# First adjacency blocks cast in halves by two engines, and engine programs outside a block, in a graph convolution with residual layer norm

## The reference

```
def reference(x, adj, t, weight):            # x 4096x256, adj 4096x4096, weight 256x256, all float32
    support = x @ weight
    y = (1 - t) * support + t * (adj @ support)
    return layernorm(x + y)                  # over the 256 features, eps 1e-5
```

## Time and profile before

| | |
|---|---|
| median of 3 runs | 384.52 us (384.37 to 384.85) |
| profiled execution, its own time | 384.54 us |
| its span, first to last instruction | 382.8 us |
| PE busy | 376.0 us (98%) |
| DVE busy | 238.5 us (62%) |
| ACT busy | 145.7 us (38%) |
| POOL busy | 22.4 us (6%) |
| moved by DMA | 84.42 MB, mean 221 GB/s |

### The profile page before, as it was taken

The page is one execution under the profiler, slowest core; times in us unless marked ns, Lnnn a source line. Parts: engine busy times, 40 slices in busy tenths (PEclk is TensorE's granted clock), DMA queues, the critical chain, the costliest instruction groups (busy, mean ns, idle before and its releaser), DMA issues.

```text
span 382.8 us, 4178 instructions
## 1 busy us (share of the span) xinstructions
PE 376.0 (98%) x1686; PEld 309.9 (81%) x1686; DVE 238.5 (62%) x335; ACT 145.7 (38%) x114; POOL 22.4 (6%) x19
## 2 busy tenths in 40 slices
PE   8999999999999999999999999999999999999994
PEld 5788888888888888888888888888888888888883
DVE  4958965446879467744577346873377643697315
ACT  4757544233352433323424324244332334523002
POOL 1201400003000010000100001000100001000000
PEclk9999999999999999999999999999999999999998
DMA  8999996556465756556655565756647567321001
GB/s 253 415 410 417 415 422 260 193 206 219 174 234 200 262 193 250 181 218 263 220 193 206 205 232 212 252 188 217 223 164 274 181 260 274 123 98 55 2 0 56
DMA packets 19107, 84.42 MB, mean 221 GB/s; under 512 B 1936, under 2 KB 6800, under 8 KB 11408
## 3 DMA queue, kind: packets, MB, share of 16 engines
q1 hardware_dynamic: 18656, 83.89, 59.6%
q10 hardware_dynamic: 432, 0.26, 0.2%
HBM read 79.95 MB, written 4.19 MB: 220 GB/s over the span
## 4 chain that ended last, share of the span: by engine, by line
PE 97%; DMA 1%; DVE 1%; ACT 0%; SPq 0%; issue 0%; DVEq 0%
PE agg L568 30%; PE agg L570 30%; PE agg L569 30%; PE out_ps L631 3%; PE out_ps L632 2%; DMA a_raw<-in_first_run 1%; PE agg L580 0%; PE agg L584 0%; PE agg L588 0%; ACT x_raw L329 0%; DVE x_raw L535 0%; DVE stats L539 0%; ACT a_hi L261 0%; PE out_ps L652 0%; PE out_ps L654 0%
## 5 line engine op out<-in xcount | busy, mean ns | idle before, releaser
L365 DVE TENSOR_TENSOR a_lo<-a_raw,a_hi 128x2048 fp32r<-128x2048 f32 x60 | 138.1, 2303 | 111.2 <-ACT a_hi L267 111.2
L568 PE MATMUL agg<-a_hi,x_hi 128*128 128x512 f32 x504 | 196.4, 390 | 0.0
L570 PE MATMUL agg<-a_hi,x_lo 128*128 128x512 f32 x504 | 196.2, 389 | 0.0
L569 PE MATMUL agg<-a_lo,x_hi 128*128 128x512 f32 x504 | 196.1, 389 | 0.0
L267 ACT ACTIVATE a_hi<-a_raw 128x2048 fp32r<-128x2048 f32 x60 | 114.7, 1913 | 128.9 <-PE agg L570 121.0
L568 PEld LDWEIGHTS agg<-a_hi,x_hi 128*128 128x128 f32 x504 | 94.6, 188 | 20.1 <-issue 0.3
L570 PEld LDWEIGHTS agg<-a_hi,x_lo 128*128 128x128 f32 x504 | 94.6, 188 | 19.9
L569 PEld LDWEIGHTS agg<-a_lo,x_hi 128*128 128x128 f32 x504 | 94.6, 188 | 19.4
L345 POOL TENSOR_TENSOR xt<-xt,omt_col 128x1024 f32<-128x1024 f32 x8 | 17.9, 2240 | 292.4 <-DMA xt<-in_xT 292.4
L631 PE MATMUL out_ps<-w_split,z_hi 128*128 128x512 f32 x56 | 20.0, 397 | 0.0
L278 ACT ACTIVATE std<-var_eps 128x4 f32<-128x4 f32 x7 | 1.4, 206 | 47.7 <-DVE var_eps L406 47.7
(11 more groups left out here) (76 smaller groups left out, 93.9 us busy)
## 6 DMA issues: line engine op xcount, KB each, us to landing
a_raw<-in_adjT SPq DMA_DIRECT2D x60, 1024.0 KB, 4.9
xt<-in_xT SPq DMA_DIRECT2D x8, 512.0 KB, 6.0
rows<-in_x SPq DMA_DIRECT2D x8, 512.0 KB, 5.7
out<-x_raw SPq DMA_DIRECT2D x7, 512.0 KB, 2.9
x_raw<-in_first_run SPq DMA_DIRECT2D x6, 512.0 KB, 12.3
a_raw<-in_first_run SPq DMA_DIRECT2D x8, 256.0 KB, 4.4
a_raw<-in_first_run SPq DMA_DIRECT2D x4, 512.0 KB, 7.2
x_raw<-in_first_run SPq DMA_DIRECT2D x4, 128.0 KB, 4.0
```

What stands on the lines that cost most here:

```text
L365: nc.vector.tensor_tensor(a_lo[:, slot], a_raw[:, slot], a_hi[:, slot].bitcast(f32), ALU.subtract).then_inc(a_lo_ready[slot], 1)
L568: nc.tensor.matmul(bank, x_hi[:, j, cols], a_hi[:, slot, b], start=first, stop=False)
L569: nc.tensor.matmul(bank, x_hi[:, j, cols], a_lo[:, slot, b], start=False, stop=False)
L570: return nc.tensor.matmul(bank, x_lo[:, j, cols], a_hi[:, slot, b], start=False, stop=last)
```

## The change

Two things are changed. In the first, the casts of pieces 1, 2 and 3 are divided as that of piece 0 was: ScalarE casts the left 256 columns, VectorE the right 256. VectorE's order becomes x0, half 0, a_lo 0, half 1, a_lo 1, x1, half 2, a_lo 2, half 3, a_lo 3, x2, a_lo 4, a_lo 5, x3, a_lo 6, a_lo 7. A semaphore half_hi_ready counts VectorE's halves; VectorE itself waits for it before the subtraction, and TensorE before each fine piece. In the second, the block is left out: the five functions lose their decorators and are called one after another with the engines. The meeting of the engines at the block's end goes with it.

```
-        first_hi_ready = sem("first_hi_ready")
+        half_hi_ready = sem("half_hi_ready")
...
-        block = ctx.enter_context(nc.Block())
-
...
-        @block.sync
-        def _(sp):
+        def load_and_store(sp):
...
-        @block.scalar
-        def _(act):
+        def scalar_engine(act):
...
             act.preload_act_table_set("sqrt_and_others")
-            act.wait_ge(a0_loaded[0], 16)
-            nc.scalar.activation(a_hi[:, 0, 0, 0:WIDE // 2], a_raw[:, 0, 0, 0:WIDE // 2], ACT.Copy
-                                 ).then_inc(a0_hi_ready, 1)
-            for q in range(1, A_EARLY):
+            for q in range(FINE):
+                slot, b, _ = A_PIECES[q]
+                act.wait_ge(a0_loaded[q], 16)
+                nc.scalar.activation(a_hi[:, slot, b, 0:WIDE // 2], a_raw[:, slot, b, 0:WIDE // 2], ACT.Copy
+                                     ).then_inc(a0_hi_ready, 1)
+            for q in range(FINE, A_EARLY):
                 a_high_piece(q)
...
-            x_high(0)
-            dve.wait_ge(a0_loaded[0], 16)
-            nc.vector.tensor_copy(a_hi[:, 0, 0, WIDE // 2:], a_raw[:, 0, 0, WIDE // 2:]).then_inc(first_hi_ready, 1)
-            dve.wait_ge(first_hi_ready, 1)
-            a_low_piece(0)
-            for p in range(1, EARLY):
-                a_low_piece(2 * p - 1)
+            def a_half_high(q):
+                slot, b, _ = A_PIECES[q]
+                dve.wait_ge(a0_loaded[q], 16)
+                nc.vector.tensor_copy(a_hi[:, slot, b, WIDE // 2:], a_raw[:, slot, b, WIDE // 2:]
+                                      ).then_inc(half_hi_ready, 1)
+                dve.wait_ge(half_hi_ready, q + 1)
+
+            for p in range(EARLY):
                 x_high(p)
-                a_low_piece(2 * p)
-            a_low_piece(A_EARLY - 1)
+                for q in (2 * p, 2 * p + 1):
+                    if q < FINE:
+                        a_half_high(q)
+                    a_low_piece(q)
...
                 pe.wait_ge(x0_hi_ready, b + 1)
                 pe.wait_ge(a0_hi_ready, q + 1)
-                if q == 0:
-                    pe.wait_ge(first_hi_ready, 1)
+                pe.wait_ge(half_hi_ready, q + 1)
...
+        load_and_store(nc.sync)
+        scalar_engine(nc.scalar)
+        pool_engine(nc.gpsimd)
+        vector_engine(nc.vector)
+        tensor_engine(nc.tensor)
```

More of the change, by code:

```diff
@@ L333, in _, with pool_engine @@
                 act.dma_start(out[c * WIDE + i * P:c * WIDE + (i + 1) * P], normed(c)[:, i]).then_inc(act_stored, 16)
-        @block.gpsimd
-        def _(pool):
+        def pool_engine(pool):
             def x_low(p):
@@ L358, in _, with vector_engine @@
                 scale_xt(c)
-        @block.vector
-        def _(dve):
+        def vector_engine(dve):
             def a_low(n):
@@ L561, in _, with tensor_engine @@
                                         ).then_inc(normed_ready, 1)
-        @block.tensor
-        def _(pe):
+        def tensor_engine(pe):
             def products(c, slot, j, b, k, first, last):
```

## The result

| | before | changed |
|---|---|---|
| median | 384.65 us (383.78 to 384.97, 14 runs) | 383.62 us (382.89 to 384.03, 14 runs) |
| ratio | | 0.9973, interval 0.9966 to 0.998 |
| profiled execution | 384.54 us | 383.16 us |
| its span | 382.8 us | 381.9 us |
| outside the span | 1.74 us | 1.26 us |

The changed kernel is faster by 1.03 us in the medians, by 0.77 to 1.31 us by the interval. The runs of either kernel spread over more than 1 us, so one profile is one draw; the table's last line is the one that doesn't scatter. Over its 14 runs the changed kernel spends 1.18 to 1.32 us outside the span. The 67 runs of the kernel before beside the experiments lie between 1.69 and 1.80 us (one more run took 1357.84 us and is left out everywhere).

The account below looks back on a forecast made before the run. TensorE was taken to bound the kernel, busy from 11 to 370 us, so only the first 11 and last 9 us could matter: 384.54 - 0.40 (barrier) - 0.00 (entry) + 0.18 (piece 4) = 384.3 us, range 383.7 to 384.8 us.

Parts of the forecast that it names:

- The end barrier inside the span: End of the span, behind SyncE's last wait: without the engines' meeting 0.40 us less, between 0.32 and 0.47 us.
- The end barrier outside the span: Behind the traced span: 1.74 us outside it, kept unchanged in the sum.
- the barrier pays twice: Rival, program end: a second engine meeting outside the span also saves 0.40 us, giving 383.7 us; chance 0.14.
- The prediction's own sign: Program end: if the time falls by clearly more than the span does, the barrier pays twice.
- The entry: Program start, before the first transfer: leaving out the block gains 0.00 us, at most 0.07 us.
- The gain of 0.21 us on piece 1: Head: halved cast takes 0.42 instead of 0.63 us, so TensorE starts piece 1 at 6.34 instead of 6.55 us.
- The loss on VectorE's run: VectorE before piece 4: added halves delay third x cast and GpSimd's x_lo; piece 4 0.18 us later, losing piece 1's 0.21.
- Rival (d): GpSimd's third x_lo loses the port over two subtractions, piece 4 0.79 us late: 384.9 us, slower; chance 0.10.
- the 0.18 us for piece 4: TensorE's piece 4 starts at 11.03 instead of 10.85 us, behind VectorE's longer run; bounds 0.00 to +0.66 us.
- The chance of 0.12 for faster by over 0.2%: Whole kernel: chance 0.12 of a measured time below 383.75 us, where 0.2% is 0.77 us.

Follow-up runs that it names:

- two halves: Changed kernel (no block) with halves for pieces 0 and 1 only, against the kernel before: 383.63 us, ratio 0.9982.
- the two delayed kernels: No block, VectorE and ScalarE held until adjacency piece 7 landed, one with old casts, one with halves of pieces 0 to 3: 392.15 and 393.01 us.
- VectorE last: Changed kernel with VectorE in SyncE's place as the one engine waiting for the last stores, against the kernel before: 383.84 us, ratio 0.9979.
- block-free with old casts: Kernel before with only the block left out, casts as before: 383.19 us, ratio 0.9966 (5 runs).
- halves with block: Kernel before with only the half casts added, block and end barrier kept: 384.43 us, ratio 0.9997.
- ScalarE last: Changed kernel with ScalarE in SyncE's place as the one engine waiting for the last stores, against the kernel before: 383.98 us, ratio 0.998.
- block-free again: Kernel before with only the block left out, casts as before, measured a second time: 383.51 us, ratio 0.9973 (7 runs).

## Why the prediction was wrong

**The end barrier inside the span: right.** I took 0.40 us from the rows of L58. The missing meeting shortened the stretch behind SyncE's wait from 0.4 us to nothing.

**The end barrier outside the span: the step that failed.** The sum was made against 1.74 us outside the span as if these were fixed, and they fell to 1.25 us: 0.49 us that stand in the sum with nothing. It had been a rival, "the barrier pays twice", priced with 0.40 us for this part against a measured 0.49 us, and with a chance of 0.14. My reason against it was that nothing in the trace shows it. That is no reason: the trace ends where the effect begins. What a trace does show is that all five engines ended together, and the change was about just that. Its mechanism I had half right: four engines do come early, but most of the gain is that GpSimd does; with the other four early and GpSimd last, 1.77 us stood outside. The prediction's own sign pointed here too: the time of the profiled run fell by 1.38 us, the span by 0.9 us.

**The entry: right**, 0.00 us; the first transfer is issued at 0.80 us in both. Whether a jump went away there isn't shown: the trace of before has one branch in all, SyncE's at the end. So the rule on taken branches in the Trainium skill (Runtime: NRT & Kernel Launch, "Instruction fetch mechanics") is neither borne out nor refuted here.

**The gain of 0.21 us on piece 1: a gain that the profile of before had, and other executions hadn't.** It needs TensorE to wait for piece 1. In the profile of before that piece was cast at 5.78 us; in the eleven other profiles it was 4.75 to 5.41 us, with piece 0 cast between 3.71 and 4.72 us. TensorE needs 1.37 us or more for piece 0, so a whole cast of 0.63 us is over in time: in all eleven TensorE started piece 1 at least 0.3 us after such a cast had ended, or would have. I built a step on a single landing. (That landing I also misread: the issue at 1.24 us is piece 0's. Piece 1 was issued at 1.71 us, where the 4.04 us of the earlier trace rows begin. Nothing hangs on it.)

**The loss on VectorE's run: right in kind, about right in size, smaller in effect.** From the a_lo of piece 1 to the third x cast, it is 2.79, 2.98 and 2.86 us with whole casts, and with halves 3.18, 3.11, 3.10 and 3.10 us in the profiles where VectorE doesn't stand waiting for a landing: +0.25 us on average, where I had 0.39 us. With whole casts VectorE stands for up to 0.2 us of that run waiting for ScalarE's cast of piece 2; in the kernel with two halves, where it doesn't, the run took 2.63 us. And piece 4 does wait for what hangs on this run: in six of twelve profiles (before, and five with halves; the two delayed kernels aren't counted) its first matmul starts 0.14 to 0.15 us after GpSimd's third x_lo ends, as in the earlier trace rows. One of them is the kernel with VectorE last. Its timeline of GpSimd:

```profile
9.55 1.18 POOL L334 TENSOR_TENSOR x_lo<-x_raw,x_hi 128x256 fp32r<-128x256 f32 x1 [2.32 <-DVE x_hi L422]
```

And of TensorE:

```profile
10.88 0.47 PE L563 MATMUL agg<-a_hi,x_hi 128*128 128x512 f32 x1 [0.23 <-POOL x_lo L334]
```

It ended at 10.73 us and TensorE started at 10.88 us. In two profiles TensorE waits for the a_lo of piece 4 (the changed kernel, behind its landing, and the first of block-free with old casts). In four it waits for nothing, because it got there late itself: piece 0 was cast only at 4.72 us (two halves), or its clock rose late, at 6.35 us (halves with block), 6.20 us (ScalarE last) and 5.10 us (block-free again), where the others have 3.75 to 4.88 us. The prediction has no such term. Piece 4 starts between 10.34 and 11.21 us over the twelve profiles, with whole casts at 10.34, 10.57 and 10.85 us. This scatter, from landings and from TensorE's clock, is larger than either step of mine, and nearly all of it arises there: from piece 4's first matmul to ScalarE's last instruction it is 368.23 to 368.28 us in the eight profiles where that matmul had to wait, and 368.12 to 368.14 us in the four where it hadn't, whichever kernel it is.

**Rival (d)**, GpSimd locked out over two subtractions: not seen. Its third x_lo took 0.74 to 1.26 us in all twelve profiles.

**Range and chances.** With 0.49 us taken off as well, my sum would have been 383.8 us, against 383.62 us; without the 0.18 us for piece 4 it would have been 383.65 us, but no run shows that this term is nothing. The chance of 0.12 for faster by over 0.2% was too small for the same reason. The interval of the ratio reaches from just that bound (0.998) downwards.

## What to carry to other kernels

A kernel's time has a part that its trace doesn't show, and a change at the end of the program should be priced there too: compare a run's time with its span, over several runs, since that difference is far steadier (here within 0.15 us) than either of them. The last wait of a kernel belongs to one engine, and which one matters: SyncE here; a meeting of all engines behind it costs once inside the span and once more by making the others late, GpSimd above all. At the start, where landings and TensorE's rising clock decide, one profile is one draw: a step of 0.2 us that rests on when a piece landed needs a second profile.

## What the runs showed of the hardware

- The time outside the span depends on which engine ends last: 1.25 us (SyncE), 1.33 (VectorE), 1.38 (ScalarE), 1.50 (TensorE), 1.77 (GpSimd), and 1.75 to 1.77 us when all end together. How the stretch is made up isn't shown.
- The same first transfers, issued at the same times within 0.03 us, landed up to 1.6 us apart: piece 0 was cast between 3.71 and 4.72 us, piece 2 between 5.77 and 7.38 us.
- With the same warming matmuls from 0.84 us on, TensorE's full clock began between 3.75 and 6.35 us in the twelve profiles; matmuls started about 0.43 us apart before and 0.23 us apart after. Where it began at 6.35 us, piece 0 took 2.35 us (4.70 to 7.05 us).
- VectorE's 128x256 cast took 0.28 to 0.29 us as a rule, but 0.73 us (6.71 to 7.44 us, the halves with block) where GpSimd's x_lo had begun at 6.55 and ran until 7.29 us. In the twelve profiles six casts are lengthened so (0.32 to 0.73 us), and each ends 0.14 to 0.16 us after GpSimd's instruction: a cast from fp32 to fp32r is held up by GpSimd just as a subtraction is. That is what the Trainium skill (SBUF — State Buffer, "SBUF: two separate sides") says of an fp32 copy; the prediction had found no row for it. The two rows, from the timelines of GpSimd and VectorE:

```profile
6.55 0.74 POOL L342 TENSOR_TENSOR x_lo<-x_raw,x_hi 128x256 fp32r<-128x256 f32 x1 [2.43 <-DVE x_hi L431]
6.71 0.73 DVE L478 CAST a_hi<-a_raw 128x256 fp32r<-128x256 f32 x1 [0.24 <-DMA a_raw<-in_first_run]
```
